# adaLN block with attention and channel mix: attention product in three fp32r parts, and the token mix split between ScalarE and VectorE

## The chip, the cores and the metric

One Trainium2 chip (trn2), one of its cores. The metric is the device time of one execution in microseconds. The kernel before took 690.93 us, the median of three runs between 690.6 and 691.36.

## The reference: what is computed

The input x is 8 batch rows of 2048 tokens of 256 numbers, all fp32. `c` (8 x 256) gives, through silu and one product with `wmod`, six vectors of 256 per batch row: shift, scale and gate for each of two halves. The reference, cut to what matters:

```python
h = _layernorm(x) * (1 + ca) + sa
qkv = h @ w_qkv + b_qkv                       # 8 heads of 64
scores = einsum('bhld,bhle->bhde', q, k) / 8  # 64 x 64 per head: attention over channels
out = einsum('bhld,bhde->bhle', v, softmax(scores)) @ w_fc + b_fc + h
x = x + ga * (layernorm(out) * gamma + beta)
h = _layernorm(x) * (1 + cb) + sb
prev = h shifted by one token, zero in front
xr = mu_r * h + (1 - mu_r) * prev
xk = mu_k * h + (1 - mu_k) * prev
x = x + gb * sigmoid(xr @ W_r.T) * (square(relu(xk @ W_k.T)) @ W_v.T)
```

## The kernel before

Since attention is over channels, everything from the layer norm to the centred output of `w_fc` and the residual is one 256 x 256 matrix m per batch row, so that the attention half is z @ m, where z is the normalised x. m comes from the Gram matrix of z over the whole batch row. The kernel therefore works on row b's second stage while it builds the Gram matrix of row n = b + 1.

The work is cut into 8 batch rows and each of these into 4 chunks (j) of 512 tokens, a chunk into 4 tiles of 128. Every engine has its own instruction stream, an order written out by hand in a function `row_steps` (row 0 with small differences, rows 1 to 6 in a loop) and `last_row` for row 7; the engines meet in semaphores. In each engine's stream a waiting instruction holds up all that is behind it. In this order PE does in a row: attention(b,0), turn_and_gram(n,0), ffn_r and ffn_k of (b-1,3), attention(b,1), ffn_out(b-1,3), turn_and_gram(n,1), turn_z2(b,0), attention(b,2), turn_and_gram(n,2), ffn_r and ffn_k (b,0), turn_z2(b,1), attention(b,3), ffn_out(b,0), turn_and_gram(n,3), turn_z2(b,2), ffn_r and ffn_k (b,1), gram_q(n), ffn_out(b,1), scores(n), ffn_r and ffn_k (b,2), wv_attn(n), turn_z2(b,3), make_m(n), ffn_out(b,2).

What happens to a chunk:
- `stats_a` (DVE, L876) and `rstd_a` (POOL, L453 to L465) give mean and inverse deviation of x; `make_z` (DVE, L886) writes z, four instructions of 255 columns.
- `turn_and_gram` (PE, L1260 and L1267) transposes z into the two PSUM banks `tr` and adds to the Gram matrix; `copy_z_t` (ACT, L620) copies the banks to `z_t`. The banks `tr` are also those of `turn_z2`.
- `attention` (PE, L1285) multiplies z_t with m_sb in fp32 into the banks `att`. It waits until DVE has read the banks of the chunk before (`t_done`).
- `squares` (ACT, L654) and `rstd_o` (POOL, L480, a pow) give the second norm, `make_x2` (DVE, L896 and L901) writes t_buf and from it x2, `stats_2` (DVE, L907) and `rstd_2` (POOL, L471 a pow, L473) the third norm, `make_z2` (ACT, L701) z2.
- `turn_z2` (PE, L1302) transposes z2, `copy_h2` (ACT, L663) writes h2 transposed into `h2t`.
- `mix` (DVE) writes dif = h2 - prev into the memory of t_buf (L930, one instruction of 1024 columns), then xr and xk by four instructions dif * mu + prev (L934).
- `ffn_r` (PE, L1318) and `take_r` (ACT, L673, tanh); `ffn_k` (PE, L1335), `take_k` (ACT, L682 relu, L684 square, L686 copy to k_hi in fp32r), `low_k` (DVE, L943) the rest k_lo; `ffn_out` (PE, L1151 to L1153) the product with w_v in three fp32r products: k_hi with the low part of the weights, k_hi with the high part, k_lo with the high part. `gate_o` (DVE, L952) and `add_y` (POOL, a DMA that adds into the output).

Once per row: `prep_base_qk` (ACT, L693, L694) and `prep_qk` (DVE, L991, L993: four instructions, each with two SBUF tensors) scale the q and k weights; `prep_wv` (POOL, L496 and L499, 1024 and 1020 columns) the v weights; `make_m` (DVE, L1026) adds the residual to the product and gives m_sb, which PE's attention of the next row and the load of the row's `ca` values by SP wait for. `take_wvf` (DVE, L972 to L977) splits the gated w_v in two fp32r parts.

Of the kernel before, what the change touches and what calls it, by code (L numbers as in the profile page):

```python
# [30 lines left out]
P = 128  # L31


def adaln_block(nc, x, w_qkv, b_qkv, w_fc, b_fc, gamma, beta, w_r, w_k, w_v, mu_r, mu_k, c, wmod, out):
# [19 lines left out]
    with ExitStack() as ctx:  # L54
# [41 lines left out]
        mu_col = sb("mu_col", [P, 2, KD])  # L96
        wv_t = sb("wv_t", [P, NP, D])
# [30 lines left out]
        m_sb = sb("m_sb", [P, KD, D])  # L128

# [3 lines left out]
        z_t = sb("z_t", [P, CH, KD, CT])  # L133
# [113 lines left out]
        m_ready = sem("m_ready")  # L247

# [7 lines left out]
        z_t_ready = sem("z_t_ready")  # L256
# [16 lines left out]
        dif_done = sem("dif_done")  # L273
# [314 lines left out]
        def _(act):  # L588
# [76 lines left out]

            def take_r(b, j, alone=False):
# [9 lines left out]
            def take_k(b, j, alone=False, halves=(0, 1)):  # L676

                i = CH * b + j
                for h in halves:
# [6 lines left out]
                    nc.scalar.activation(k_split(j)[0][:, h], k[:], ACT.Copy).then_inc(k_hi_ready, 1)  # L686
# [18 lines left out]
            def row_steps(b, first):  # L705
# [803 lines left out]
```

## Time and profile before

| what | before |
|---|---|
| median of the runs | 690.93 us |
| the profiled execution's own time | 690.6 us |
| its span, first to last instruction | 688.9 us |
| PE busy | 670.7 us (97%) |
| DVE busy | 561.0 us (81%) |
| ACT busy | 393.8 us (57%) |
| POOL busy | 317.5 us (46%) |
| TensorE clock granted, mean | 0.991 |
| attention of row 0, 1, 4 and 7 starts at | 57.98, 131.04, 371.72, 612.36 us |

A busy time is the part of the span in which the engine had an instruction in work; a PE that is busy need not be at its peak. In the timelines a line merges instructions of one kind that follow each other: start, length of the whole, engine, source line, operation, what is written from what, form, and x how many. In square brackets stands how long the engine sat idle before and whose end released it. PE's records show an fp32 product twice and an fp32r product once. Successive records overlap, so that the start of the next group, not the end of a record, tells when PE was free.

### The profile page before, as it was taken

The numbers are of one execution on the slowest core, as the hardware profiler recorded it, in microseconds if no ns is written. First come the engines' busy times: TensorE is split into PE (matmuls) and PEld (weight loads), VectorE is DVE, ScalarE is ACT, GpSimd is POOL, SyncE is SP. The second block draws the span as 40 slices with busy tenths as digits, with TensorE's granted clock in tenths as the row PEclk, the third lists the DMA queues.
The fourth block names the chain that finished last, engine by engine and source line by source line (L and its number), as shares of the span: only waits on it lengthen the run. The fifth ranks groups of instructions, "written<-read, shape, count | busy, mean of one in ns | idle before, by whom it ended". The sixth has DMA issues, their size and how long they took to land.

```text
span 688.9 us, 11754 instructions
## 1 busy us (share of the span) xinstructions
PE 670.7 (97%) x3712; PEld 539.4 (78%) x3712; DVE 561.0 (81%) x1254; ACT 393.8 (57%) x871; POOL 317.5 (46%) x520
## 2 busy tenths in 40 slices
PE   7988999999999999999999999999999999999896
PEld 6777886888778887879868887788878788687674
DVE  5693999789887998889887898979988898658973
ACT  1424575566754675474855667546754747547662
POOL 5272864573254642565335742646325753214320
PEclk9989999999999999999999999999999999999999
DMA  8849345485836666572855849366665528628225
GB/s 316 232 152 222 103 131 123 77 212 97 209 74 142 163 135 147 99 167 92 198 113 79 219 91 213 67 141 158 145 136 99 107 72 173 123 37 179 37 31 91
DMA packets 90984, 93.02 MB, mean 135 GB/s; under 512 B 4224, under 2 KB 89000, under 8 KB 90960
## 3 DMA queue, kind: packets, MB, share of 16 engines
q0 software_dynamic: 33264, 33.03, 32.6%
q1 hardware_dynamic: 55344, 55.97, 25.6%
q10 hardware_dynamic: 2352, 3.73, 1.5%
q8 instruction: 11, 0.18, 0.1%
q14 instruction: 13, 0.11, 0.0%
HBM read 42.84 MB, written 33.10 MB: 110 GB/s over the span
## 4 chain that ended last, share of the span: by engine, by line
PE 86%; DVE 7%; POOL 2%; DMA 2%; issue 1%; ACT 1%; SPq 0%; DVEq 0%; POOLq 0%
PE work L1335 14%; PE work L1318 14%; PE att L1285 13%; PE gram L1267 11%; PE gram L1398 4%; PE att L1370 4%; PE work L1151 4%; PE tr L1260 4%; PE work L1153 4%; PE work L1152 4%; PE tr L1302 4%; PE att L1389 2%; PE gram L1380 1%; PE att L1318 1%; DVE st L907 1%
## 5 line engine op out<-in xcount | busy, mean ns | idle before, releaser
L471 POOL TENSOR_TENSOR rs<-ve,neg_half 128x4 f32<-128x4 f32 x32 | 41.6, 1300 | 161.4 <-DVE ve L917 161.4
L1285 PE MATMUL att<-m_sb,z_t 128*128 128x256 f32 x496 | 112.4, 380 | 1.6 <-issue 0.8
L1335 PE MATMUL work<-mx,w_k_t 128*128 128x512 f32 x236 | 106.2, 592 | 0.0
L1285 PEld LDWEIGHTS att<-m_sb,z_t 128*128 128x128 f32 x496 | 92.4, 190 | 16.9 <-issue 5.7
L1318 PE MATMUL work<-w_r_t,mx 128*128 128x256 f32 x464 | 105.7, 381 | 0.0
L1318 PEld LDWEIGHTS work<-w_r_t,mx 128*128 128x128 f32 x464 | 85.9, 190 | 11.1
L1267 PE MATMUL gram<-z 128*128 128x256 f32 (+1 forms) x512 | 90.7, 331 | 0.0
L1267 PEld LDWEIGHTS gram<-z 128*128 128x128 f32 x512 | 81.1, 194 | 6.9
L934 DVE SCALAR_TENSOR_TENSOR mx<-t_buf,mu_col,h2t 128x512 f32<-128x512 f32 x120 | 84.3, 765 | 1.1
L654 ACT ACTIVATE sq<-att 128x256 f32<-128x256 f32 x124 | 46.1, 383 | 64.1 <-PE att L1285 64.1
L1335 PEld LDWEIGHTS work<-mx,w_k_t 128*128 128x128 f32 x236 | 44.8, 190 | 44.1 <-issue 42.6
L701 ACT ACTIVATE z<-x,nm,rs 128x256 f32<-128x256 f32 x128 | 66.5, 600 | 21.5 <-POOL nm L473 21.2
L1151 PE MATMUL work<-wvf_lo,k_hi 128*128 128x256 f32 x248 | 75.5, 304 | 1.4 <-issue 1.0
L896 DVE SCALAR_TENSOR_TENSOR t_buf<-att,rs_o,g_row 128x256 f32<-128x256 f32 x124 | 51.4, 477 | 27.8 <-POOL rs_o L480 26.9
L886 DVE TENSOR_SCALAR z<-x_in,ag_a 128x255 f32<-128x255 f32 x128 | 65.1, 570 | 5.1 <-POOL ag_a L465 3.6
L673 ACT ACTIVATE y<-work 128x512 f32<-128x512 f32 x58 | 34.5, 595 | 60.6 <-PE work L1318 60.5
L1153 PE MATMUL work<-wvf_hi,k_lo 128*128 128x256 f32 x248 | 68.9, 278 | 0.0
L1152 PE MATMUL work<-wvf_hi,k_hi 128*128 128x256 f32 x248 | 68.8, 277 | 0.0
L943 DVE TENSOR_TENSOR k_lo<-work,k_hi 128x512 fp32r<-128x512 f32 x61 | 41.2, 688 | 32.0 <-ACT k_hi L686 31.7
L663 ACT ACTIVATE h2t<-tr,mod_now 128x512 f32<-128x512 f32 x64 | 46.3, 778 | 16.0 <-PE tr L1302 16.0
L485 POOL DMA_DIRECT2D x<-in_L_attn_x_dram x32 | 55.2, 1825 | 0.0
L512 POOL DMA_DIRECT2D out_dram<-y x29 | 39.3, 1355 | 34.1 <-DVE y L952 33.7
(170 smaller groups left out, 1283.6 us busy)
## 6 DMA issues: line engine op xcount, KB each, us to landing
x_in<-in_L_attn_x_dram SPq DMA_DIRECT2D x32, 512.0 KB, 4.8
x<-rows SPq DMA_DIRECT2D x32, 512.0 KB, 3.4
x<-in_L_attn_x_dram POOLq DMA_DIRECT2D x32, 512.0 KB, 8.9
out_dram<-x SPq DMA_DIRECT2D x31, 512.0 KB, 5.1
out_dram<-y POOLq DMA_DIRECT2D x29, 512.0 KB, 6.2
rows<-row_scratch SPq DMA_DIRECT2D x16, 128.0 KB, 4.1
rows<-row_scratch SPq DMA_DIRECT2D x8, 256.0 KB, 3.8
wqkv_sb<-in_L_attn_w_qkv_dram ACTq DMA_DIRECT2D x1, 1536.0 KB, 9.7
```

What stands on the lines that cost most here:

```text
L485: nc.gpsimd.dma_start(x2[:, j], x_v[b, j], accum_op=ALU.add).then_inc(x2_filled[j], 16)
L701: ins = nc.scalar.activation(z2[:, t], x2[:, j, t], ACT.Identity, bias=nm_2[:, s, t:t + 1], scale=rs_2[:, s, t:t + 1])
L886: ins = nc.vector.tensor_scalar(z[:, j % 2, t, 0:LAST], x_in[:, j, t, 0:LAST], ag_a[:, j, 3, t:t + 1], ag_a[:, j, 7, t:t + 1], ALU.subtrac ...
L896: ins = nc.vector.scalar_tensor_tensor(t_buf[:, t], att_banks(j, alone)[t // 2][:, (t % 2) * D:(t % 2 + 1) * D], rs_o[:, s, t:t + 1], g_ro ...
L934: ins = nc.vector.scalar_tensor_tensor(dst[:, h], dif[:, h], mu_col[:, n, h:h + 1], prev[:, h], ALU.mult, ALU.add)
L1151: mm(dst, s_hi, m_lo, start=start, stop=False)
L1152: mm(dst, s_hi, m_hi, start=False, stop=False)
L1153: return mm(dst, s_lo, m_hi, start=False, stop=stop)
L1267: ins = mm(gram[:, k * D:(k + 1) * D - k * P], z[:, j % 2, t, k * P:(k + 1) * P], z[:, j % 2, t, k * P:D], start=(j == 0 and t == 0 and k ...
L1285: ins = mm(att_banks(j, alone)[q][:, (t % 2) * D:(t % 2 + 1) * D], z_t[:, j, k, t * P:(t + 1) * P], m_sb[:, k], start=(k == 0), stop=(k == ...
L1318: ins = mm(r_banks(alone)[q][:, (t % 2) * D:(t % 2 + 1) * D], mixed(j, alone)[0][:, ch, tile], w_r_t[:, ch], start=(ch == 0), stop=(ch == ...
L1335: ins = mm(k_banks(alone)[dh][:], w_k_t[:, ch, rows_dh], mixed(j, alone)[1][:, ch], start=(ch == 0), stop=(ch == KD - 1))
```

## The change

- **Attention in three products.** z_t becomes z_hi, a copy in fp32r by ACT (`copy_z_hi`), and z_lo, the rest, by DVE (`low_z`, two instructions of 512 columns per chunk, from the banks `tr`). m_sb is split by DVE into m_hi (a cast) and m_lo (a subtraction), 512 columns each, once per row. `attention` does the three products of `mm3` for each tile. Who waited for z_t_ready now waits for z_lo_ready, turn_z2 half by half.
- **The mix.** ACT writes mu * h2 into xr and xk (`scale_h2`, four instructions of 512 columns per chunk, right behind copy_h2, for j = 1 behind squares(b,3)), and DVE adds (1 - mu) * prev in place (four instructions per chunk). dif and its instruction are gone, and so are the waits of make_x2 and take_wvf for the memory shared with it. 1 - mu is worked out once (`make_rest`).
- **The order on DVE** in rows 1 to 6: make_z(n,2) and low_k(b-1,3) now stand before prep_qk(n), which stood before them.
- k_hi and k_lo have one buffer instead of two; in the last row chunks 2 and 3 use xr and xk instead of z_t, and the last k takes z_hi.

```diff
-        z_t = sb("z_t", [P, CH, KD, CT])
+        z_hi, z_lo = (part(n, [P, CH, KD, CT]) for n in ("z_hi", "z_lo"))
-        k_hi, k_lo = (part(n, [P, 2, KD, CT]) for n in ("k_hi", "k_lo"))
+        k_hi, k_lo = (part(n, [P, KD, CT]) for n in ("k_hi", "k_lo"))
...
+            def scale_h2(b, j):
+
+                i = CH * b + j
+                wait_past(act, r_done, 2 * i - 2)
+                wait_past(act, k_done, 2 * i - 2)
+                act.wait_ge(h2_ready, 2 * i + 2)
+                for n, (dst, scaled) in enumerate(zip(mixed(j), (xr_scaled, xk_scaled))):
+                    for h in range(KD):
+                        nc.scalar.activation(dst[:, h], h2t[:, h, 1 + j * CT:1 + (j + 1) * CT], ACT.Copy,
+                                             scale=mu_col[:, n, h:h + 1]).then_inc(scaled, 1)
...
                 copy_h2(b, 0)
+                scale_h2(b, 0)
...
                 copy_h2(b, 1)
                 squares(b, 3)
+                scale_h2(b, 1)
                 make_z2(b, 2)
-                copy_z_t(n, 3)
+                copy_z_hi(n, 3)
                 copy_gram(n)
                 copy_gram_low(n)
                 copy_h2(b, 2)
+                scale_h2(b, 2)
...
                 copy_h2(b, 3)
+                scale_h2(b, 3)
...
-                nc.vector.tensor_tensor(dif, h2t[:, :, 1 + j * CT:1 + (j + 1) * CT], prev, ALU.subtract).then_inc(dif_done, 1)
-                dve.wait_ge(dif_done, i + 1)
-                for n, (dst, ready) in enumerate(zip(mixed(j, alone), (xr_mixed, xk_mixed))):
+                parts = (xr_scaled, xr_mixed), (xk_scaled, xk_mixed)
+                for n, (dst, (scaled, ready)) in enumerate(zip(mixed(j), parts)):
+                    dve.wait_ge(scaled, 2 * i + 2)
                     for h in range(KD):
-                        ins = nc.vector.scalar_tensor_tensor(dst[:, h], dif[:, h], mu_col[:, n, h:h + 1], prev[:, h],
+                        ins = nc.vector.scalar_tensor_tensor(dst[:, h], prev[:, h], rest_col[:, n, h:h + 1], dst[:, h],
                                                              ALU.mult, ALU.add)
                     ins.then_inc(ready, 1)
+
+            def low_z(b, j):
+
+                i = CH * b + j
+                for h in range(KD):
+                    dve.wait_ge(z_hi_ready, 2 * i + h + 1)
+                    nc.vector.tensor_tensor(z_lo[:, j, h], tr[h][:], z_hi[:, j, h].bitcast(F32),
+                                            ALU.subtract).then_inc(z_lo_ready, 1)
...
                 nc.vector.tensor_tensor(m_sb[:].rearrange("p k d -> p (k d)"), gram[:],
-                                        res[:].rearrange("p k d -> p (k d)"), ALU.add).then_inc(m_ready, 1)
+                                        res[:].rearrange("p k d -> p (k d)"), ALU.add).then_inc(m_step, 1)
+                dve.wait_ge(m_step, 2 * b + 1)
+                nc.vector.tensor_copy(m_hi[:], m_sb[:]).then_inc(m_step, 1)
+                dve.wait_ge(m_step, 2 * b + 2)
+                nc.vector.tensor_tensor(m_lo[:], m_sb[:], m_hi[:].bitcast(F32), ALU.subtract).then_inc(m_ready, 1)
...
                 prep_now(n)
+                low_z(n, 0)
                 make_x2(b, 0)
                 stats_2(b, 0)
                 if first:
                     stats_a(n, 2)
                     stats_a(n, 3)
+                    low_z(n, 1)
                     make_x2(b, 1)
                     stats_2(b, 1)
                     make_z(n, 2)
                 else:
+                    make_z(n, 2)
+                    low_k(b - 1, 3)
                     prep_qk(n)
-                    low_k(b - 1, 3)
-                    make_z(n, 2)
+                    low_z(n, 1)
                     make_x2(b, 1)
                     stats_2(b, 1)
                 mix(b, 0)
+                low_z(n, 2)
...
                 mix(b, 1)
+                low_z(n, 3)
                 gate_o(b, 0)
...
-                            ins = mm(att_banks(j, alone)[q][:, (t % 2) * D:(t % 2 + 1) * D], z_t[:, j, k, t * P:(t + 1) * P], m_sb[:, k],
-                                     start=(k == 0), stop=(k == KD - 1))
+                            ins = mm3(att_banks(j, alone)[q][:, (t % 2) * D:(t % 2 + 1) * D],
+                                      (z_hi[:, j, k, tile], z_lo[:, j, k, tile], m_hi[:, k], m_lo[:, k]),
+                                      start=(k == 0), stop=(k == KD - 1))
...
-                elif not last and j < CH - 1:
-                    pe.wait_ge(z_t_ready, 2 * (i + 1 + CH) + 2)
-                else:
+                elif last or j == CH - 1:
                     wait_past(pe, h2_ready, 2 * i)
                 for h in range(KD):
+                    if not last and j < CH - 1:
+                        pe.wait_ge(z_lo_ready, 2 * (i + 1 + CH) + 1 + h)
```

## Rows read from the trace of the kernel before

**Rows 1.** Windows: busy us by engine, batch row 4 and the last row:
```profile
371.72:451.91 80.19, 80.16 (x451) 65.04 (x450) 68.62 (x153) 48.68 (x108) 38.53 (x63) 1.00 0.63 137
612.36:688.90 76.54, 67.21 (x338) 51.91 (x336) 54.65 (x117) 42.46 (x96) 22.68 (x23) 0.98 0.42 76
```

**Rows 2.** Timeline of PE, row 4: start us, us, engine, what, count:
```profile
371.72 3.62 PE L1285 MATMUL att<-m_sb,z_t 128*128 128x256 f32 x16
375.18 1.04 PE L1260 MATMUL tr<-ident,z 128*128 128x128 f32 x8
...
396.42 3.62 PE L1285 MATMUL att<-m_sb,z_t 128*128 128x256 f32 x16
...
406.83 3.60 PE L1335 MATMUL work<-mx,w_k_t 128*128 128x512 f32 x8
...
414.94 0.28 PE L1151 MATMUL work<-wvf_lo,k_hi 128*128 128x256 f32 x1
...
415.28 0.28 PE L1151 MATMUL work<-wvf_lo,k_hi 128*128 128x256 f32 x1
...
420.82 1.04 PE L1302 MATMUL tr<-ident,z 128*128 128x128 f32 x8
```

**Rows 3.** Timeline of ACT in row 4:
```profile
407.52 2.06 ACT L701 ACTIVATE z<-x,nm,rs 128x256 f32<-128x256 f32 x4
...
415.69 2.10 ACT L701 ACTIVATE z<-x,nm,rs 128x256 f32<-128x256 f32 x4
417.96 1.08 ACT L620 ACTIVATE z_t<-tr 128x512 f32<-128x512 f32 x2 [0.17 <-PE tr L1260]
```

**Rows 4.** Groups of ACT by line and shape: busy us, mean ns, idle before:
```profile
L663 ACT ACTIVATE h2t<-tr,mod_now 128x512 f32<-128x512 f32 x64 | 46.3, 778 | 16.0 <-PE tr L1302 16.0
...
L620 ACT ACTIVATE z_t<-tr 128x512 f32<-128x512 f32 x64 | 34.7, 598 | 30.8 <-PE tr L1260 19.2 <-issue 11.5
...
L693 ACT ACTIVATE wqk_aug<-wqk_last,neg_d 128x1024 f32<-128x1024 f32 x8 | 9.2, 1154 | 1.4 <-DVE d_now L984 1.4
...
L694 ACT ACTIVATE res<-ident_c,d_now 128x256 f32<-128x256 f32 x8 | 4.0, 500 | 0.0
```

**Rows 5.** Groups of DVE by line and shape, same columns:
```profile
L943 DVE TENSOR_TENSOR k_lo<-work,k_hi 128x512 fp32r<-128x512 f32 x61 | 41.2, 688 | 32.0 <-ACT k_hi L686 31.7
...
L930 DVE TENSOR_TENSOR t_buf<-h2t 128x1024 f32<-128x1024 f32 x32 | 39.1, 1220 | 6.0 <-ACT h2t L663 4.1 <-PE work L1318 0.8 <-DVE x L901 0.5
...
L975 DVE CAST wvf_hi<-t_buf 128x512 fp32r<-128x512 f32 x7 | 3.3, 476 | 0.2
```

**Rows 6.** Timeline of DVE in row 4:
```profile
384.69 1.28 DVE L991 SCALAR_TENSOR_TENSOR wqk_aug<-wqkv_sb,d_now,wqk_aug 128x1024 f32<-128x1024 f32 x1
...
394.14 1.66 DVE L896 SCALAR_TENSOR_TENSOR t_buf<-att,rs_o,g_row 128x256 f32<-128x256 f32 x4 [1.18 <-POOL rs_o L480]
```

**Rows 7.** Timeline of DVE at 389 us, and the second z alone:
```profile
389.08 3.88 DVE L886 TENSOR_SCALAR z<-x_in,ag_a 128x255 f32<-128x255 f32 x4
...
390.27 2.04 DVE L886 TENSOR_SCALAR z<-x_in,ag_a 128x255 f32<-128x255 f32 x1
```

**Rows 8.** Timeline of POOL in row 4:
```profile
384.87 1.99 POOL L471 TENSOR_TENSOR rs<-ve,neg_half 128x4 f32<-128x4 f32 x1 [2.70 <-DVE ve L917]
...
387.58 2.62 POOL L496 TENSOR_TENSOR wv_aug<-wv_t,rows 128x1024 f32<-128x1024 f32 x1
390.28 1.89 POOL L499 TENSOR_TENSOR wv_aug<-wv_aug 128x1020 f32<-128x1020 f32 x1
...
393.10 1.01 POOL L480 TENSOR_TENSOR rs_o<-ve_o,neg_half 128x4 f32<-128x4 f32 x1
```

**Rows 9.** Timeline of DVE at the start of row 0:
```profile
57.19 0.69 DVE L1026 TENSOR_TENSOR m_sb<-gram,res 128x512 f32<-128x512 f32 x1 [5.48 <-PE gram L1398]
...
63.81 0.15 DVE L983 TENSOR_SCALAR neg_d<-rows 128x1 f32<-128x1 f32 x1 [5.66 <-DMA rows<-row_scratch]
```

**Rows 10.** Timeline of PE at the second attention chunk of row 0:
```profile
65.79 3.69 PE L1285 MATMUL att<-m_sb,z_t 128*128 128x256 f32 x16 [0.62 <-DVE t_buf L896]
```

More of the change, by code:

```diff
@@ L162, in y_buf, with k_split, mixed @@
             return x_in[:, j] if alone else y[:, j % 2]
-        def k_split(j):
-            return k_hi[:, j % 2], k_lo[:, j % 2]
+        def k_split(j, alone):
+            return (z_hi[:, 0], z_hi[:, 1]) if alone and j == CH - 1 else (k_hi, k_lo)
         def o_banks(j, alone):
             return att if alone and j == CH - 1 else work[0:2]
-        def mixed(j, alone):
-            return (z_t[:, 2 * j - CH], z_t[:, 2 * j - CH + 1]) if alone and j >= CH // 2 else (xr[:, j % 2], xk[:, j % 2])
+        def mixed(j):
+            return xr[:, j % 2], xk[:, j % 2]
         wmod_sb = h2t[:, :, 1:1 + 6 * D]
@@ L619, in copy_z_t @@
                     act.wait_ge(z_turned, 2 * i + h + 1)
-                    nc.scalar.activation(z_t[:, j, h], tr[h][:], ACT.Copy).then_inc(z_t_ready, 1)
+                    nc.scalar.activation(z_hi[:, j, h], tr[h][:], ACT.Copy).then_inc(z_hi_ready, 1)
             def copy_gram(b):
@@ L752, in last_row @@
                 copy_h2(b, 0)
+                scale_h2(b, 0)
                 make_z2(b, 1)
@@ L755, in last_row @@
                 copy_h2(b, 1)
+                scale_h2(b, 1)
                 take_r(b, 0)
@@ L760, in last_row @@
                 copy_h2(b, 2)
+                scale_h2(b, 2)
                 take_r(b, 1, alone=True)
@@ L764, in last_row @@
                 copy_h2(b, 3)
+                scale_h2(b, 3)
                 take_r(b, 2, alone=True)
@@ L888, in make_z, with make_x2 @@
                 ins.then_inc(z_ready, 1)
-            def make_x2(b, j, mixes=None, alone=False):
+            def make_x2(b, j, alone=False):
                 i, s = CH * b + j, j % 2
-                wait_past(dve, xk_mixed, CH * b + (max(j - 1, 0) if mixes is None else mixes))
+                wait_past(dve, x2_ready, i)
                 dve.wait_ge(rs_o_ready, i + 1)
@@ L1085, in last_row @@
                 stats_2(b, 0)
[L1086 removed]
+                make_x2(b, 1, alone=True)
                 stats_2(b, 1)
                 low_k(b - 1, 3)
[L1089 to L1090 removed]
+                make_x2(b, 2, alone=True)
+                mix(b, 0)
                 gate_o(b - 1, 3)
                 stats_2(b, 2)
[L1093 to L1094 removed]
+                mix(b, 1)
+                make_x2(b, 3, alone=True)
                 take_wvf(b, alone=True)
@@ L1097, in last_row @@
                 stats_2(b, 3)
-                mix(b, 2, alone=True)
+                mix(b, 2)
                 gate_o(b, 0)
                 low_k(b, 1, alone=True)
-                mix(b, 3, alone=True)
+                mix(b, 3)
                 gate_o(b, 1, alone=True)
@@ L1116, in _ @@
             make_z(0, 1, first=True)
+            low_z(0, 0)
             stats_a(0, 3)
@@ L1120, in _ @@
             prep_now(0)
+            low_z(0, 1)
             make_z(0, 3, first=True)
@@ L1123, in _ @@
             prep_qk(0)
+            low_z(0, 2)
             rows_b()
+            low_z(0, 3)
             centre_fc()
+            make_rest()
             stats_a(1, 0)
```

71 lines of the change are left out of this document (35 added, 36 removed).

## The prediction

> **What bounds the kernel now.** I read the windows first, batch row by batch row, then the waits of PE, then the timelines of one middle row. The window of row 4 [rows 1] shows PE busy for 80.16 of its 80.19 us, DVE for 68.62 and ACT for 48.68: PE is the bound in rows 1 to 6, and everything else has slack in front of it. The last row is different: PE works 67.21 of 76.54 us, so a chain through several engines sets its end. A PE that is full says what a shorter product could give at most; what it will give is decided by how much slack each hand-over had. So I wrote down for row 4, with 371.72 as zero, when PE comes to each wait and when the buffer is ready, and did the same for the new order. The points that matter are: attention(b,2) starts at 24.70 (396.42 in [rows 2]), its bank is free when t_buf of chunk 1 is done, 394.14 + 1.66 = 395.80 or 24.08 [rows 6]; ffn_r(b,0) ends and ffn_k(b,0) starts at 35.11 (406.83), and turn_z2(b,2) starts at 49.10 (420.82) [rows 2].
>
> **PE's own work.** An attention chunk takes from 371.72 to 375.18 [rows 2], 3.46 us: 16 records of fp32. The new one is 24 records like those of lines 1151 to 1153, of which three take 415.28 - 414.94 = 0.34 us [rows 2], so 2.72 us: 0.74 less. Four chunks a row make 2.96, all 32 chunks 23.7 us. Were nothing else changed, that would be the gain.
>
> **ACT's added work.** scale_h2 is four activations per chunk, SBUF to SBUF, 512 wide, with a pointer scale. None stands in the trace. The two neighbours in kind are 1154 ns at 1024 columns and 500 ns at 256 [rows 4], a straight line between them gives 718 ns at 512; successive ones overlap by about 0.1 us (the two z_t copies of 598 ns take 1.08 together [rows 3, 4]), so 0.62 each, 2.48 for four, 9.9 us a row. Bounds: 0.49 each if it goes like the plain copy from PSUM, 0.67 if like h2t's 778 ns [rows 4]. ACT has 31.5 us a row free, so in sum it is covered; in one place it is not. After ffn_r(b,0) ACT does, without a gap, the second tanh (to 407.52), make_z2(b,1), relu, square and copy of both halves, copy_h2(b,1), squares(b,3) (to 415.69), make_z2(b,2) and then z_t for the next row's chunk 3, which waits 0.17 for PE [rows 3]. The new queue puts scale_h2(b,1) between squares(b,3) and make_z2(b,2), and turn_z2(b,2) no longer waits for the copy but for low_z, DVE's subtraction behind it. From the end of ffn_r(b,0): 0.69 + 8.17 (407.52 to 415.69) + 2.48 + 2.0 (make_z2) + 0.60 (first half of z_hi) + 0.69 (low_z, priced as k_lo [rows 5]) + 0.1 for hand-overs = 14.73 us. PE used to take 420.82 - 406.83 = 13.99, and would take 13.25. So from ffn_r(b,0) to turn_z2(b,2) the row gets 0.74 longer than before. This eats exactly the 0.74 that attention(b,2) gives between its start and ffn_r's end. What is left: **the row changes by as much as the start of attention(b,2) moves**. Behind turn_z2(b,2) I find no wait that lengthens it: m needs a cast and a subtraction more, 0.48 + 0.69 [rows 5], ready at about 79.65 in old offsets, while PE is in ffn_out(b,2) to 80.19.
>
> **The start of attention(b,2).** By PE's work alone it would move from 24.70 to 23.2. It waits for t_buf of chunk 1, which was ready 0.6 before it, at 24.08, and which does not hang on the attention product: it hangs on mix(b-1,3), the row start of DVE, POOL's chain for rs_o, then POOL's two wide operations of prep_wv. The start of this chain in the row stays (mix is four operations instead of five, 1.22 us less [rows 5], behind an m that comes 1.2 later). low_z(n,0), 1.3 us, falls in DVE's wait for rs_o(b,0). With the rest unchanged attention(b,2) starts at 24.15, 0.55 earlier.
> But the rest changes: prep_qk moves from before low_k to behind it, and make_z(n,2) in front. Today prep_qk starts at 384.69 and is past before POOL begins the wide 2.62 us at 387.58; it is make_z that runs beside it, and the rows show what happens: its four instructions take 3.88 us, the second alone 2.04, from 390.27 to just behind the end of POOL's 1.89 us operation at 392.17 [rows 7, 8]. They wait for POOL to be through. The two that are left of the four take 0.66. Conversely POOL's pow takes 1.99 beside prep_qk and 1.01 at 393.10 where DVE is idle [rows 8]: prep_qk and POOL hinder each other too. The Trainium skill says this against the change (GPSIMD Engine Reference, Key points): GpSimd shares its SBUF interfaces with VectorE, with contention for instructions in a two-port mode or with two SBUF inputs, which takes in both make_z and prep_qk. By that rule the trace agrees for make_z; for prep_qk only the 1.99 bears on it.
> From the rows, in the new order: make_z from 13.0 to 14.35, low_k(b-1,3) from 14.4 to 15.85 (its second half waits for ACT), POOL's wide operation from about 14.7 to 17.3. prep_qk's first instruction comes at 15.85 into it and ends at about 18.3. If the two engines then alternate, POOL's second wide one ends at 20.2 and prep_qk at 22.0, low_z(n,1) (1.3) at 23.3, t_buf at 24.95: attention(b,2) at 25.05, later by 0.35. If DVE goes first, prep_qk ends at 20.6 but POOL at 22.2, rs_o at 24.05, t_buf at 25.7: later by 1.1. Bounds: 23.2 (no wait at all, 1.5 earlier) and 26.2 (1.5 later). I take 0.4 later, near the alternating case, since the rows show both sides getting a turn: six rows cost 2.4 us.
>
> **Prologue and row 0.** In front of row 0 PE waits for m [rows 9], so cast and subtraction cost their 1.2 in full. low_z of the first four chunks puts 5.1 us on DVE; two of the four fall in waits for ACT and DMA, the other two, with the slack before the score softmax, push wv_attn by about 0.9. The row of ca is loaded only once m is ready, and DVE waits 5.66 for it (63.81) [rows 9]; then low_z(1,0), 1.3, stands ahead of make_x2(0,0), whose t_buf attention(0,1) waits for already now [rows 10]. It starts 3.4 later. low_z(1,1) in front of make_x2(0,1) adds 1.3, of which the shorter product and waits leave 0.6; make_z(1,2) behind it brings the first stage to 4.75 late, and ACT's chain keeps it so. Bounds 2 and 5.5; I take 4.75.
> **Last row.** The shorter products bring attention(b,2) forward by 2.2 us and its rs_o with it; mix loses the difference (1.22) but waits for ACT's scaling. Following DVE from there I keep 1.4 of it to the end; bounds 0 and 3.
>
> **Sum.** The profiled execution took 690.6 us, span 688.9, 1.7 around it; it lies 0.3 under the median 690.93. 690.6 + 4.75 + 2.4 - 1.4 = 696.35, and 0.3 to the median: **696.7 us**. A measurement of this kernel tells about 0.2%, 1.4 us, from no change.
>
> **The rivals.**
> Forecast, chance 0.40: 693 to 700.
> No port cost: prep_qk slides between POOL's operations, attention(b,2) is 0.55 earlier. 690.93 + 4.75 - 3.3 - 1.4 = 691.0, chance 0.18. For it: only make_z is seen blocked, and prep_qk's own 1.28 us is the same beside pow.
> **Faster by a quicker ACT.** Place: ACT's queue between squares(b,3) and z_hi(n,3). If scaling goes at 0.49, each row gains 0.52 more; with no port cost 1.07 a row, with prologue at 2: 690.93 + 2 - 6.4 - 1.4 = 685.1, chance 0.20. It decides at z_hi(n,3) plus low_z ready 13.25 us behind ffn_r(b,0): under that PE is the bound again.
> The waits are all absorbed, because DVE and ACT run ahead of PE more than I see: 23.7 less, 667, chance 0.07. Against it: DVE's t_buf at 24.08 in the row is fixed by engines other than PE.
> Port at its worst, 1.1 a row, start 5.5, last row 0: 690.93 + 5.5 + 6.6 = 703.0, chance 0.15.
> That the products don't get shorter is no case: the same three products run in ffn_out at 0.34 a triple.
>
> **How the numbers follow.** Faster by over 0.2%: 0.27 and 0.04 of the no-port case, 0.31. Within: 0.10, all of it from that case. Slower: 0.40 + 0.15 + 0.04 = 0.59. The range runs from the quick ACT's 685 to the worst port's 703; outside are 667 and the tails, under 0.2 together. The slower cases alone run from 693 to 703.
>
> **What would show it.** Right: attention chunks of 2.7 us; PE busy about 77 of a row of 80.6; waits of PE at turn_z2 for DVE's z_lo, and at attention for t_buf; prep_qk's group at line 991 with a mean well over 1.28 us, and z's under 0.57. Four scalings near 2.5 us. attention(0,0) some 2 us later. Wrong: a middle row under 79.5 us, or line 991 still at 1.28, or PE waiting mostly in another place, above all ffn_out for k_lo.

## The result, and the profile after

The changed kernel takes 698.39 us (median of four runs, 697.56 to 699.25) against 690.91 us of the kernel before beside it: 1.0108 times as long, 95% interval 1.009 to 1.0125. The profiled execution took 699.25 us with a span of 697.6, so 8.7 more than the span of before; between the medians it is 7.5. PE is busy for 659.2 us (before 670.7), DVE for 569.9 (561.0), ACT for 469.3 (393.8), POOL for 313.0 (317.5).

Where the 8.7 us come from is read from the starts of attention(b,0): row 0 at 59.52 (before 57.98), row 1 at 138.59 (131.04), row 7 at 621.82 (612.36). So the prologue costs 1.54, row 0 another 6.01, rows 1 to 6 together 1.91, and the last row gives 0.76 back. The first of these is the least certain: in the kernels below whose prologue is the changed kernel's, row 0 starts anywhere from 58.05 to 60.84. The windows of row 4 and of the last row, as in [rows 1] (length, then busy us of PE, weight loads, DVE, ACT, POOL, then clock, DMA share, GB/s):

```profile
380.28:460.87 80.59, 78.48 (x484) 64.74 (x482) 69.70 (x160) 57.99 (x124) 38.61 (x63) 1.00 0.62 137
621.82:697.60 75.78, 65.85 (x370) 52.88 (x368) 49.87 (x112) 52.28 (x112) 20.70 (x23) 0.95 0.43 77
```

PE, which had 0.03 us free in a row before, now has 2.11, and the row is 0.40 longer. Two of PE's waits, summed over the span (us, times, longest), name both places:

```profile
PE tr L1348 <- DVE z_lo L965: 9.5, 7, 2.8
PE att L1195 <- DVE t_buf L920: 8.2, 8, 1.4
```

The timeline of PE in row 4 shows them one by one (compare [rows 2]):

```profile
380.28 0.28 PE L1195 MATMUL att<-m_lo,z_hi 128*128 128x256 f32 x1
...
383.15 1.04 PE L1304 MATMUL tr<-ident,z 128*128 128x128 f32 x8
...
404.83 0.36 PE L1195 MATMUL att<-m_lo,z_hi 128*128 128x256 f32 x1 [1.00 <-DVE t_buf L920]
...
414.72 3.60 PE L1381 MATMUL work<-mx,w_k_t 128*128 128x512 f32 x8
...
421.90 0.28 PE L1195 MATMUL work<-wvf_lo,k_hi 128*128 128x256 f32 x1
...
424.62 1.04 PE L1304 MATMUL tr<-ident,z 128*128 128x128 f32 x8
...
429.39 1.25 PE L1348 MATMUL tr<-ident,z 128*128 128x128 f32 x8 [1.11 <-DVE z_lo L965]
```

An attention chunk takes 383.15 - 380.28 = 2.87 us instead of 3.46. Offsets in a row are counted from the start of its attention(b,0), here 380.28. Attention(b,2) starts at 24.55 in the row (before 24.70), although PE stood ready 1.00 earlier. From ffn_k(b,0) to turn_z2(b,2) it is 14.67 (before 13.99). The first wait is explained by DVE's timeline in front of it, with prep_qk in its new place (compare [rows 6]):

```profile
395.60 0.69 DVE L973 TENSOR_TENSOR k_lo<-work,k_hi 128x512 fp32r<-128x512 f32 x1 [0.48 <-ACT k_hi L701]
396.21 2.09 DVE L1020 SCALAR_TENSOR_TENSOR wqk_aug<-wqkv_sb,d_now,wqk_aug 128x1024 f32<-128x1024 f32 x1
398.22 2.10 DVE L1022 SCALAR_TENSOR_TENSOR res<-last_c,neg_d,res 128x256 f32<-128x256 f32 x1
400.25 1.27 DVE L1020 SCALAR_TENSOR_TENSOR wqk_aug<-wqkv_sb,d_now,wqk_aug 127x1024 f32<-127x1024 f32 x1
401.44 0.47 DVE L1022 SCALAR_TENSOR_TENSOR res<-last_c,neg_d,res 127x256 f32<-127x256 f32 x1
401.84 1.28 DVE L965 TENSOR_TENSOR z_lo<-tr,z_hi 128x512 fp32r<-128x512 f32 x2
403.04 1.65 DVE L920 SCALAR_TENSOR_TENSOR t_buf<-att,rs_o,g_row 128x256 f32<-128x256 f32 x4
```

and POOL's timeline beside it (compare [rows 8]):

```profile
394.81 2.41 POOL L500 TENSOR_TENSOR wv_aug<-wv_t,rows 128x1024 f32<-128x1024 f32 x1
397.29 2.75 POOL L503 TENSOR_TENSOR wv_aug<-wv_aug 128x1020 f32<-128x1020 f32 x1
```

The two engines take turns, and each seems to wait for the other to be through with a whole instruction. DVE's first one starts at 396.21, inside POOL's L500 that ends at 397.22, and ends at 398.30, 1.08 behind that, where alone it takes 1.27. POOL's L503 takes 2.75 where it takes 1.89 alone [rows 8], and ends at 400.04, 1.74 behind DVE's first. DVE's second instruction, 256 columns, needs 2.10 instead of 0.47 and ends at 400.32, 0.28 behind POOL. Each of the three ends 0.15 to 0.2 earlier than a full wait would have it, so the exclusion covers all but some 0.2 us of an instruction, as far as POOL's spans, which are rough in a profile, can tell. In DVE's groups (busy us, mean ns, idle) the two shapes of one line stand side by side: the first, 128 partitions, meets POOL in rows 1 to 6, the second, 127 partitions, does not.

```profile
L956 DVE SCALAR_TENSOR_TENSOR mx<-h2t,rest_col,mx 128x512 f32<-128x512 f32 x128 | 91.3, 775 | 18.9 <-ACT mx L678 18.9
L910 DVE TENSOR_SCALAR z<-x_in,ag_a 128x255 f32<-128x255 f32 x128 | 50.1, 453 | 4.7 <-POOL ag_a L469 3.5 <-PE gram L1311 0.9
...
L1020 DVE SCALAR_TENSOR_TENSOR wqk_aug<-wqkv_sb,d_now,wqk_aug 128x1024 f32<-128x1024 f32 x8 | 15.0, 1876 | 0.0
L1022 DVE SCALAR_TENSOR_TENSOR res<-last_c,neg_d,res 128x256 f32<-128x256 f32 x8 | 13.6, 1698 | 0.0
L1020 DVE SCALAR_TENSOR_TENSOR wqk_aug<-wqkv_sb,d_now,wqk_aug 127x1024 f32<-127x1024 f32 x8 | 10.2, 1274 | 0.0
```

The second wait comes from ACT's queue; its timeline in row 4 (compare [rows 3]) shows the scaling of chunk 1 ahead of z2 and z_hi:

```profile
423.59 2.59 ACT L678 ACTIVATE mx<-h2t,mu_col 128x512 f32<-128x512 f32 x4
426.04 2.08 ACT L716 ACTIVATE z<-x,nm,rs 128x256 f32<-128x256 f32 x4
428.00 1.09 ACT L624 ACTIVATE z_hi<-tr 128x512 fp32r<-128x512 f32 x2
```

Row 0 has a meeting of its own, which the prediction did not see. It is in the kernel before too, whose DVE and POOL timelines show mix(0,1) beside prep_wv:

```profile
95.81 4.84 DVE L934 SCALAR_TENSOR_TENSOR mx<-t_buf,mu_col,h2t 128x512 f32<-128x512 f32 x4
...
97.40 2.70 POOL L496 TENSOR_TENSOR wv_aug<-wv_t,rows 128x1024 f32<-128x1024 f32 x1
```

Four such instructions take 2.74 elsewhere, so 2.1 us were lost there already, and PE did not feel it: its turn_z2(0,2), at 99.85, needed ACT's copy and nothing that stood behind the mix on DVE. In the changed kernel the mix waits for ACT's scaling and starts 2.5 later, so that all four meet POOL, and z_lo, which turn_z2 now waits for, stands behind it. DVE's timeline there:

```profile
98.29 6.48 DVE L956 SCALAR_TENSOR_TENSOR mx<-h2t,rest_col,mx 128x512 f32<-128x512 f32 x4 [0.86 <-ACT mx L678]
104.69 1.28 DVE L965 TENSOR_TENSOR z_lo<-tr,z_hi 128x512 fp32r<-128x512 f32 x2
```

POOL's at the same time:

```profile
98.54 2.73 POOL L500 TENSOR_TENSOR wv_aug<-wv_t,rows 128x1024 f32<-128x1024 f32 x1
101.35 2.21 POOL L503 TENSOR_TENSOR wv_aug<-wv_aug 128x1020 f32<-128x1020 f32 x1
```

and PE's, which waits for the z_lo behind that mix and, inside ffn_r(0,1), for a gate_o that stands behind both (5.30 instead of 3.62):

```profile
105.52 1.16 PE L1348 MATMUL tr<-ident,z 128*128 128x128 f32 x8 [2.80 <-DVE z_lo L965]
...
106.62 5.30 PE L1364 MATMUL work<-w_r_t,mx 128*128 128x256 f32 x16
```

Turn_z2(0,2) is 5.67 late (105.52 against 99.85) where ffn_k(0,0) was 2.8 late (88.02 against 85.20).

### The profile page after: what moved, and what is told of

The parts are those of the page before. It is cut to its first block, busy times and chain, and to the rows that moved or that the text cites. A ratio compares the mean times of both kernels' runs of the same rounds, so it can differ in the third digit from the quotient of the medians.

```text
span 697.6 us, 12487 instructions
## 1 busy us (share of the span) xinstructions
PE 659.2 (94%) x3968; PEld 539.3 (77%) x3968; DVE 569.9 (82%) x1303; ACT 469.3 (67%) x999; POOL 313.0 (45%) x520
## 4 chain that ended last, share of the span: by engine, by line
PE 67%; ACT 16%; DVE 11%; issue 3%; DMA 1%; POOL 0%; ACTq 0%; DVEq 0%; POOLq 0%
PE work L1364 15%; PE work L1381 10%; PE gram L1311 7%; PE gram L1444 4%; ACT z L716 4%; PE att L1416 4%; PE tr L1348 3%; PE work L1195 2%; PE work L1196 2%; PE work L1197 2%; PE tr L1304 2%; PE att L1195 2%; ACT work L699 2%; PE att L1435 2%; DVE res L1022 2%
## 5 line engine op out<-in xcount | busy, mean ns | idle before, releaser
L1381 PE MATMUL work<-mx,w_k_t 128*128 128x512 f32 x244 | 109.9, 592 | 0.0
L1364 PE MATMUL work<-w_r_t,mx 128*128 128x256 f32 x464 | 109.0, 389 | 0.0
L475 POOL TENSOR_TENSOR rs<-ve,neg_half 128x4 f32<-128x4 f32 x32 | 37.6, 1175 | 154.2 <-DVE ve L941 154.1
L956 DVE SCALAR_TENSOR_TENSOR mx<-h2t,rest_col,mx 128x512 f32<-128x512 f32 x128 | 91.3, 775 | 18.9 <-ACT mx L678 18.9
L1364 PEld LDWEIGHTS work<-w_r_t,mx 128*128 128x128 f32 x464 | 88.2, 195 | 12.0
L678 ACT ACTIVATE mx<-h2t,mu_col 128x512 f32<-128x512 f32 x128 | 82.4, 723 | 2.8
L1195 PE MATMUL att<-m_lo,z_hi 128*128 128x256 f32 x248 | 74.2, 299 | 10.2 <-DVE t_buf L920 8.2
L1196 PE MATMUL att<-m_hi,z_hi 128*128 128x256 f32 x248 | 70.1, 283 | 0.0
L1197 PE MATMUL att<-m_hi,z_lo 128*128 128x256 f32 x248 | 70.0, 282 | 0.0
L1195 PEld LDWEIGHTS att<-m_lo,z_hi 128*128 128x128 f32 x248 | 47.3, 191 | 13.9 <-issue 13.9
```

What stands on the lines that cost most here:

```text
L678: nc.scalar.activation(dst[:, h], h2t[:, h, 1 + j * CT:1 + (j + 1) * CT], ACT.Copy, scale=mu_col[:, n, h:h + 1]).then_inc(scaled, 1)
L956: ins = nc.vector.scalar_tensor_tensor(dst[:, h], prev[:, h], rest_col[:, n, h:h + 1], dst[:, h], ALU.mult, ALU.add)
L1195: mm(dst, s_hi, m_lo, start=start, stop=False)
L1196: mm(dst, s_hi, m_hi, start=False, stop=False)
L1197: return mm(dst, s_lo, m_hi, start=False, stop=stop)
L1364: ins = mm(r_banks(alone)[q][:, (t % 2) * D:(t % 2 + 1) * D], mixed(j)[0][:, ch, tile], w_r_t[:, ch], start=(ch == 0), stop=(ch == KD - 1))
```

## The experiments

Ratios are against the kernel before, run on the same chip. In kernels that add or drop a line the line numbers shift by one or two.

**1. The two halves of the change alone.** att_only keeps the change's attention but leaves the mix as it was (dif on DVE, no scaling on ACT); mix_only puts the new mix into the kernel before.

Att_only, against the changed kernel (with the mix come back the waits of make_x2 and take_wvf for the memory that dif shares with t_buf):

```diff
-                scale_h2(b, 0)
...
+                nc.vector.tensor_tensor(dif, h2t[:, :, 1 + j * CT:1 + (j + 1) * CT], prev, ALU.subtract).then_inc(dif_done, 1)
...
-                        ins = nc.vector.scalar_tensor_tensor(dst[:, h], prev[:, h], rest_col[:, n, h:h + 1], dst[:, h],
+                        ins = nc.vector.scalar_tensor_tensor(dst[:, h], dif[:, h], mu_col[:, n, h:h + 1], prev[:, h],
```

Mix_only has the same lines with the signs turned round, against the kernel before; chunks 2 and 3 of its last row keep the memory of z_t.

> The changed kernel with the mix as it was before: dif and four scalar_tensor_tensor on DVE, no scale_h2 on ACT; the attention product, low_z, the split of m and DVE's new order stay. Theory (ACT's scaling lengthens the way from ffn_r(b,0) to turn_z2(b,2) to 14.7 us, and m's split delays the start of DVE's row): the wait of PE at turn_z2(b,2) goes (that way back to about 13.4 us), but mix(b-1,3) is 1.2 us longer again, so attention(b,2) starts about 1 us later than in the changed kernel. A middle row of 79.5 to 80.3 us and a total of 692 to 696. Rival (the loss comes from the attention split itself, the scaling is harmless): total 698 to 702, turn_z2(b,2) as late as in the changed kernel.

Measured: 705.16 us (703.79 to 705.97), ratio 1.0199 [1.0174, 1.0224]: 9 above the range, and 3 above that of the rival, which is nearer: the loss comes from the attention split. Its chain through ACT is short, as the theory has it (ffn_k(b,0) to turn_z2(b,2) 13.40), and its rows are 81.47 long all the same; row 0 is 7.2 longer than before, rows 1 to 6 together 7.5. PE's waits say why:

```profile
PE att L1175 <- DVE t_buf L900: 8.8, 9, 1.6
PE work L1344 <- DVE y L963: 5.5, 6, 0.9
PE tr L1328 <- DVE z_lo L946: 4.6, 7, 3.0
PE work L1175 <- DVE k_lo L954: 3.2, 6, 0.6
```

DVE, busy for 74.47 of an 81.0 us window of row 4, is late everywhere: ffn_r(b,0) waits inside for gate_o and takes 4.67. With the mix of before, the attention product in three parts costs 14 us; the new mix is what makes room on DVE for low_z. How much of this is the longer work of DVE and how much the waits for t_buf's memory is not separated.

> The kernel before with the new mix alone: scale_h2 on ACT at the new places, DVE adds in place; attention stays one fp32 product, DVE's order and k's two buffers as before. Theory (ACT's queue is full between ffn_r(b,0) and the copy of the next row's z, chunk 3): turn_z2(b,2) comes 14.5 us behind the end of ffn_r(b,0) in place of 13.99, so a row is 0.4 to 0.6 us longer, total 693 to 695. Rival (ACT has 31 us a row free, the scaling is hidden): row at 80.2, total 690.5 to 691.5 or a little under through the shorter mix of the last row.

Measured: 691.55 us (690.67 to 692.45), ratio 1.0005 [0.9996, 1.0015], less than expected and next to the rival's 690.5 to 691.5. Ffn_k(b,0) to turn_z2(b,2) is 14.43, as the theory has it, but rows 1 to 6 are only some 0.3 longer each, 1.9 together, of which the last row gives 0.9 back, and the total can't be told from before. So the scaling is not hidden, as the rival has it; its cost is small. The costs of the two halves, 14.3 and 0.7, do not add up to the 7.5 of both.

**2. The order on DVE.** order_old puts prep_qk back ahead of low_k and make_z.

```diff
-                    make_z(n, 2)
-                    low_k(b - 1, 3)
                     prep_qk(n)
+                    low_k(b - 1, 3)
+                    make_z(n, 2)
```

> The changed kernel with DVE's loop in the order of before: prep_qk, low_k, make_z, then low_z(n,1). Theory of the shared port: prep_qk is back at 1.28 us an instruction (now 2.09 and 2.10 for the first two), but make_z runs beside POOL's two wide operations again and takes 3.9 us in place of 1.38, and low_k comes 1.8 us later, so ffn_out(b-1,3) waits: attention(b,2) starts 0.3 to 0.6 us later, total 700 to 702. Rival (no port, the new order just came with a cost): both groups at their short times, total under 697.

Measured: 697.94 us (697.46 to 698.69), ratio 1.0099 [1.0077, 1.0121]: the changed kernel's time, not the 700 to 702 expected. Prep_qk's two lines are back at 1278 and 480 ns, and z's mean rises from 453 to 569: four of them take 3.88 beside POOL, as in [rows 7]. Attention(b,2) starts at 24.54, as in the changed kernel, and PE's wait of 1.14 stands ahead of ffn_out(b-1,3), for k_lo, instead of ahead of attention(b,2). So the new order is neither gain nor loss: it only chooses who meets POOL's wide operations.

**3. ACT's queue.** z_first puts z_hi(n,3) ahead of the scaling of chunk 1, and low_z(n,3) ahead of its mix.

```diff
                 squares(b, 3)
-                scale_h2(b, 1)
                 make_z2(b, 2)
                 copy_z_hi(n, 3)
+                scale_h2(b, 1)
...
-                mix(b, 1)
                 low_z(n, 3)
+                mix(b, 1)
```

> The changed kernel with ACT's scale_h2(b,1) behind copy_z_hi(n,3) and DVE's low_z(n,3) before mix(b,1). Theory (scaling ahead of z_hi(n,3) is what turn_z2(b,2) waits for): turn_z2(b,2) comes 13.3 to 13.5 us behind the end of ffn_r(b,0) (now 14.67); then PE waits for copy_gram behind the scaling, so of the 1.3 about 0.5 us a row stay: total 694 to 696. Rival (another wait ends at the same time): turn_z2(b,2) moves by under 0.3 us, total 698.

Measured: 690.65 us (688.76 to 692.13), ratio 0.9996 [0.9983, 1.0009], better than expected. Ffn_k(b,0) to turn_z2(b,2) is 13.39, what PE's own work takes, and rows are 79.6 to 79.8. Row 0 is 3.9 shorter: low_z(1,3) no longer stands behind mix(0,1), and turn_z2(0,2) comes at 43.28 in the row instead of 46.00. Mix(0,1) meets only the end of POOL's operations (3.30 instead of 6.48), but it also starts 3.99 later in its row, and ends later. Turn_z2(b,2) is no longer late; PE then waits up to 0.6 for ACT's copy of the Gram matrix and for xr.

**4. POOL's wide operations, moved.** row0_wv_late moves prep_wv of row 0 behind rstd_2(0,3); wv_late moves that of rows 1 to 6 behind rstd_o(b,2).

Row0_wv_late:

```diff
-                if first:
-                    prep_wv(n)
                 add_y(b, 0)
                 fill_x2(n, 0)
                 rstd_2(b, 3)
+                if first:
+                    prep_wv(n)
```

Wv_late:

```diff
-                    prep_wv(n)
                     rstd_o(b, 1)
                     rstd_2(b, 1)
                     rstd_o(b, 2)
+                    prep_wv(n)
```

> The changed kernel with POOL's two wide operations of row 0 (prep_wv) moved from before add_y(0,0) to behind rstd_2(0,3); rows 1 to 7 as they are. Theory (in row 0 they hold the port while DVE does mix(0,1), which takes 6.48 us there and 2.73 elsewhere, and low_z(1,3) and gate_o(0,0) stand behind it): mix(0,1) is back at 2.7 us, turn_z2(0,2) 2.5 to 3 us and ffn_k(0,1) 4 to 5 us earlier, row 0 at 74 to 75 us in place of 79.07, total 693 to 695. Rival (mix(0,1) is slow through something else, the added stores of ACT in the same stretch for one): row 0 stays at 79, total 698.

Measured: 696.26 us (695.81 to 697.19), ratio 1.0079 [1.0062, 1.0096], 2 less than the changed kernel where 4 to 5 were expected. Turn_z2(0,2) comes at 43.04 in the row instead of 46.00, ffn_k(0,1) at 47.60 instead of 52.25: the meeting with mix(0,1) did cost 3 to 4.6 us. But row 0 is only 3.1 shorter, 75.98: behind the wide operations stands rstd_a of the next rows, z comes late, k_lo behind it, and make_m to ffn_out(0,2) takes 5.01 instead of 3.35.

> The changed kernel with POOL's two wide operations of rows 1 to 6 moved behind rstd_o(b,2), where DVE does low_z, gate_o and take_wvf. Theory (they and prep_qk shut each other out, and t_buf of chunk 1 is late by it): the four instructions of prep_qk take 3.5 us (now 5.7), rs_o(b,1) no longer stands behind them, attention(b,2) starts at 23.4 to 23.8 in its row (now 24.55) and the row is 0.8 to 1.1 us shorter: total 691.5 to 693.5. Rival (attention(b,2) has another bound at nearly the same time): under 0.3 us a row, 696.5 to 698.

Measured: 697.33 us (695.38 to 698.35), ratio 1.0081 [1.0062, 1.01]: a miss. The time is in the rival's range, but not for the rival's reason: attention(b,2) starts at 23.20, PE's own time, so its wait was the meeting of prep_qk with POOL. The meeting only moves on to take_wvf, in DVE's timeline of row 4:

```profile
411.03 1.62 DVE L1001 TENSOR_TENSOR t_buf<-w_v_t,rows 128x512 f32<-128x512 f32 x1
412.68 2.00 DVE L1004 CAST wvf_hi<-t_buf 128x512 fp32r<-128x512 f32 x1
414.70 0.69 DVE L1006 TENSOR_TENSOR wvf_lo<-t_buf,wvf_hi 128x512 fp32r<-128x512 f32 x1
...
420.55 1.28 DVE L973 TENSOR_TENSOR k_lo<-work,k_hi 128x512 fp32r<-128x512 f32 x2
```

The product L1001 takes 0.68 and the cast 0.43 to 0.48 where POOL is quiet. Attention(b,3) then waits 0.28 for t_buf, and ffn_out(b,0) longer, in PE's timeline:

```profile
421.93 0.36 PE L1195 MATMUL work<-wvf_lo,k_hi 128*128 128x256 f32 x1 [1.49 <-issue]
```

The view names no releaser, but k_lo, which ffn_out waits for and which stands on DVE behind the late work, is done at 421.83. A row keeps only 0.5 of the 1.35.

> The changed kernel with three moves together: scale_h2(b,1) behind copy_z_hi(n,3) with low_z(n,3) before mix(b,1), prep_wv late in row 0 and late in rows 1 to 6. If the three losses are separate links of one chain their gains add: rows of 78.4 to 78.9 us, row 0 at 74 to 75, total 683 to 686, faster than both kernels. Rival (taking one away uncovers the next): 688 to 690.

Measured, experiments 3 and 4 together: 694.87 us (694.33 to 696.68), ratio 1.0058 [1.0043, 1.0074]: a miss of both ranges, worse than z_first alone. Attention(b,2) at 23.20, but attention(b,3) at 37.86, ffn_out(b,0) at 42.45 and turn_z2(b,2) at 48.85. The loss is wv_late's wait ahead of ffn_out(b,0), 1.50 here. It alone puts turn_z2(b,2) there (48.84 in wv_late); PE waits for no z_lo in the rows of either kernel. So getting z_lo early gains nothing here, while ffn_r(b,1) now comes 1.34 behind turn_z2(b,2) instead of 0.98, because ACT's copy of the Gram matrix stands behind the scaling.

Combo_split cuts the scaling and the mix of chunk 1 in combo in two:

```diff
                 copy_z_hi(n, 3)
-                scale_h2(b, 1)
+                scale_h2(b, 1, parts=(0,))
                 copy_gram(n)
+                scale_h2(b, 1, parts=(1,))
                 copy_gram_low(n)
...
                 low_z(n, 3)
-                mix(b, 1)
+                mix(b, 1, halves=(0,))
                 gate_o(b, 0)
+                mix(b, 1, halves=(1,))
```

> combo with scale_h2(b,1) and mix(b,1) cut in two: ACT scales xr, copies the Gram matrix, then scales xk; DVE mixes xr, does gate_o(b,0), then mixes xk. Theory (in the kernel with the scaling moved alone PE waits 0.6 us in each row for the copy of the Gram matrix behind the scaling): that wait goes, a row is 0.4 to 0.7 us shorter than in combo, total 679 to 683. Rival (ffn_r or ffn_k of chunk 1 then waits for the mix instead): no shorter than combo.

Measured: 698.5 us (698.1 to 699.71), ratio 1.0112 [1.0097, 1.0127]: a miss; the rival, no shorter than combo, holds. Ffn_r(b,1) does follow turn_z2(b,2) at once (48.93 to 49.91), but ffn_k(b,1) takes 4.00 until the next product instead of 3.43: its second half waits for ACT's tanh (y L689), which stands behind the scalings. In these two kernels the gains do not add; the wide operations still lie beside take_wvf on DVE, which reads two SBUF tensors and casts.

**5. POOL's wide operations where DVE leaves them alone.** After mix(b,2) DVE does k_lo (one operand in PSUM) and statistics (one operand), some 5 us, and POOL is idle. wv_quiet puts prep_wv there in every row and holds it until mix(b,2) is through; combo2 is wv_quiet with z_first; combo2_split also puts ACT's copies of the Gram matrix between the scaling of xr and that of xk, with the mix in one piece behind them.

```diff
-                    prep_wv(n)
                     rstd_o(b, 1)
...
-                if first:
-                    prep_wv(n)
                 add_y(b, 0)
                 fill_x2(n, 0)
+                pool.wait_ge(xk_mixed, CH * b + 3)
+                prep_wv(n)
                 rstd_2(b, 3)
```

> The changed kernel with POOL's two wide operations for the v weights moved in every row to behind the residual fill of the next row's chunk 0, and held there until DVE is through with mix(b,2); DVE then does k_lo and statistics, which take one SBUF tensor each. If it is the meeting of the two engines at prep_qk (and at mix(0,1) in row 0) that costs, prep_qk's 1024 wide instructions are back at 1.28 us each, attention(b,2) starts at about 23.2 in the row instead of 24.55, row 0 is about 3 us shorter, and rows 1 to 6 by about 1 each: 688 to 690.5 us. The rival, that the wide operations cost wherever they stand because POOL's small ones behind them come late (as in the two kernels that moved them before), gives 695 to 698.

Measured: 686.52 us (685.57 to 687.72), ratio 0.9923 [0.9909, 0.9937], 1.5 below the range. Rows are 79.16, row 0 74.77 (4.3 shorter), attention(b,2) at 23.20. Prep_qk's mean in DVE's groups is back:

```profile
L955 DVE SCALAR_TENSOR_TENSOR mx<-h2t,rest_col,mx 128x512 f32<-128x512 f32 x128 | 87.6, 747 | 19.1 <-ACT mx L677 19.0
...
L1019 DVE SCALAR_TENSOR_TENSOR wqk_aug<-wqkv_sb,d_now,wqk_aug 128x1024 f32<-128x1024 f32 x8 | 10.2, 1276 | 0.0
L1021 DVE SCALAR_TENSOR_TENSOR res<-last_c,neg_d,res 128x256 f32<-128x256 f32 x8 | 3.8, 479 | 0.0
```

> The same move together with z_hi(n,3) and z_lo(n,3) in front of the scaling and the mix of chunk 1. If the two delays (ACT's queue ahead of turn_z2(b,2), and the shared port ahead of attention(b,2)) are separate and each now has cover, the gains add: attention(b,2) at 23.2, turn_z2(b,2) at about 46.6, rows of 78.4, total 681 to 684 us, faster than both kernels. The rival (gains do not add, as in the kernel that put the wide operations behind rstd_o(b,2)): 688 to 692.

Measured: **681.58 us** (680.32 to 681.65), ratio 0.9849 [0.9836, 0.9862], faster than both kernels and as the theory has it. The window of row 4:

```profile
369.60:447.86 78.26, 77.81 (x483) 64.53 (x482) 67.53 (x160) 58.00 (x124) 36.63 (x63) 1.00 0.65 141
```

POOL's timeline shows the two wide operations undisturbed in the new place:

```profile
425.40 2.36 POOL L500 TENSOR_TENSOR wv_aug<-wv_t,rows 128x1024 f32<-128x1024 f32 x1 [2.26 <-DVE mx L955]
427.84 1.89 POOL L503 TENSOR_TENSOR wv_aug<-wv_aug 128x1020 f32<-128x1020 f32 x1
```

and DVE's beside them runs at its usual times (k_lo 0.69, four statistics 1.40):

```profile
426.71 0.69 DVE L972 TENSOR_TENSOR k_lo<-work,k_hi 128x512 fp32r<-128x512 f32 x1 [0.79 <-ACT k_hi L700]
427.31 1.40 DVE L930 BATCH_NORM_STATS2 st<-x 128x6 f32<-128x256 f32 x4
```

Only a small tensor_scalar at the end of POOL's second operation (neg L939) takes 0.53 instead of 0.17. PE is busy for all but 0.45 of the row: the 2.36 that four shorter chunks give (4 x 0.59) arrive as 80.19 - 78.26 = 1.93. Row 0 is still 2.6 longer than before (75.65 against 73.06); what is left there was not looked into.

> The kernel of the run before with ACT's copies of the Gram matrix between the scaling of xr and that of xk for chunk 1. PE waits there about 0.45 for the copy of the Gram matrix and then goes on to ffn_r(b,1), which needs only xr. If that wait is what is left, each row gets 0.3 to 0.45 shorter: 2 to 3 us less than the run before. If DVE's gate_o(b,0), which comes 0.8 later behind the mix of xk, sets ffn_out or the second Gram product, the time is the same or up to 2 us more.

Measured: 693.06 us (691.49 to 694.88), ratio 1.002 [1.0008, 1.0032]: 14 above the gain that was expected and 9 above the worst case. Ffn_r(b,1) starts 0.39 earlier, and its second half waits for gate_o(b,0), which stands on DVE behind the mix of xk, and that waits for ACT's later scaling. PE's timeline in row 4:

```profile
425.73 1.99 PE L1365 MATMUL work<-w_r_t,mx 128*128 128x256 f32 x8
429.25 1.99 PE L1365 MATMUL work<-w_r_t,mx 128*128 128x256 f32 x8 [1.53 <-DVE y L983]
```

**6. The same move without the change.** before_wv_quiet is the kernel before with prep_wv moved in the same way.

> The kernel before with the same move of POOL's two wide operations and nothing else: it tells whether the move alone would have made the kernel before faster, or whether it only pays together with the shorter attention product. There PE is busy for 80.16 of the 80.19 us of a row and no wait for t_buf or prep_qk stands in front of attention(b,2), so my theory gives nothing in the rows and at most some tenths in row 0: 689.5 to 691.5 us. If POOL's wide operations cost in the kernel before as well, about 1 us per row, it gives 684 to 687, and then most of what the combined kernel gains does not come from the change.

Measured: 690.23 us (689.18 to 691.79), ratio 1.0001 [0.9992, 1.0011], as expected; rows 80.18. The move alone gives nothing where PE is the bound, and 12 us (698.39 to 686.52) in the changed kernel: 8.2 in rows 1 to 6, where t_buf had become the bound, and 4.3 in row 0, where it was z_lo behind mix(0,1); the last row takes 1.4 back. So combo2's 1.5% does not come from the move by itself, and z_first's places exist only in the changed kernel. It is the change's gain, once the two things that ate it are away.

## Why the prediction came out as it did

The time (696.7 forecast, 698.39 measured) and the sign were right, and so was the mechanism in rows 1 to 6: a shorter product whose gain late buffers take back. But most of the loss lies in row 0, and most of that has a reason that the prediction does not have; some luck is in the total as well: 5.75 more was forecast and 7.5 measured between the medians (8.7 in the profiled executions). By its steps:

- **PE's own work.** 0.74 less per chunk forecast, 0.59 measured. The step took the triple at 0.34 us from ffn_out; with z as the weights a triple takes 0.35 to 0.36.
- **ACT's added work.** 718 ns and 2.48 for four forecast; 723 ns and 2.57 to 2.59 measured. The chain from ffn_k(b,0) to turn_z2(b,2) was 14.73 forecast and 14.67 measured, and z_first (13.39) shows that the place in the queue, not the amount of work, is its cause. The Trainium skill (ScalarE: Activation LUTs, What ACT_TABLE_LOAD costs) gives 186 ns + 0.833 ns per column, 93 ns more per pointer operand and an overlap of 93 ns; for 512 columns that is 706 ns, and the trace agrees within 3%.
- **The start of attention(b,2).** Forecast 0.4 later, measured 0.15 earlier. Prep_qk ran from 15.93 to 21.63 in the row (forecast 15.85 to 22.0), in the alternating case; the error is in the tail, t_buf ready at 24.4 instead of 24.95. Experiments 2, 4 and 5 show the mechanism from three sides: move either party and the wait moves with the meeting, and it goes when there is none. The Trainium skill (SBUF — State Buffer, Who interferes with whom) calls it a lock that the first to issue holds for its whole instruction, against GpSimd reads for DVE instructions with two SBUF inputs, and against casts and tensor_scalar in a two-port mode; the 2.09, 2.75 and 2.10 us above, the cast of 2.00 and the undisturbed k_lo and statistics all agree with that, up to the 0.2 us by which each ended early.
- **Behind turn_z2(b,2)** the row was forecast unchanged and is 0.39 longer (31.48 against 31.09 to its end). "I find no wait that lengthens it" is nearly true: 0.22 of it lies in turn_z2(b,2), whose second half waits for the second half of z_lo, and 0.09 each in ffn_out(b,1) and ffn_out(b,2), which run at a slower pace without a wait.
- **The row as a whole.** Rows 1 to 6 came out at 0.32 longer on average (forecast 0.4), and that is luck. In row 4 the start of attention(b,2) was 0.55 earlier than forecast, the way from there to ffn_k(b,0) got 0.52 shorter instead of 0.74, the way to turn_z2(b,2) 0.68 longer instead of 0.74, and the rest 0.39 longer instead of 0; the four errors cancel.
- **Prologue and row 0.** Forecast 4.75, measured 7.55: the term that was mis-sized. The prologue itself was forecast about 2 and took 1.54, and attention(0,1) came 1.76 late, not 3.4. The step then said that ACT's chain keeps the lateness so; in fact ffn_k(0,0) was only 2.8 late, and then mix(0,1), all of it beside POOL's prep_wv of row 0, took 6.48, with z_lo and gate_o(0,0), which PE waits for, behind it. The meeting could be read from the trace of before, where the four took 4.84 and nothing of PE's hung on them. I had weighed that meeting for prep_qk only, because prep_qk was what the diff moved, and had not asked what else was now at that time. Row0_wv_late (the mix back at 2.74, turn_z2(0,2) 2.96 earlier) and z_first (z_lo ahead of the mix, row 0 3.9 shorter) show it.
- **Last row.** Forecast 1.4 less, measured 0.76 less; not followed further.
- **The rivals.** "No port cost" fell (prep_qk's mean is 1876 ns where it meets POOL), and its 691.0 is not the time of a kernel without the meeting either: wv_quiet takes 686.52, with rows 1.05 shorter than before instead of 0.55 and a row 0 only 1.7 longer. The quicker ACT did not come (four scalings in 2.57 to 2.59, not 4 x 0.49), but its place was right, as z_first shows. The port at its worst, 1.1 a row, did not come: attention(b,2) was early. "All absorbed", 667, did not come even in combo2.

## What to carry to other kernels

When an edit frees the bounding engine, list the buffers that were ready just before they were needed (here t_buf 0.6 us ahead): they are the next bound, and what hinders them costs from then on what it did not cost before. A meeting that costs nothing today is in today's trace: mix(0,1) at 4.84 instead of 2.74 was there to be seen. GpSimd's wide operations cost nothing in the kernel before and 12 us in the changed one; beside VectorE work with one SBUF operand or a PSUM operand, held there with a wait, they cost next to nothing here. Test such edits together as well as alone: three of the combinations here lost what their parts had gained, and one kept it.

## What the runs showed of the hardware

- The fp32r product of 128x256 has more than one pace at a granted clock of 1.00. In row 4 of the changed kernel 24 of them take 2.87 us in attention (380.28 to 383.15, 119.6 ns each) and 2.72 in ffn_out(b,0) (421.90 to 424.62, 113 ns each), with the same shapes and types. The slower pace came with z_hi and z_lo as weights in every kernel here that has them, and parts of ffn_out go at 118 ns, between the two. The cause is open; no run was made on it.
- POOL's and DVE's exclusion holds by whole instructions, but for some 0.2 us, and lets the two alternate: one DVE instruction of 0.47 us took 2.10, and a POOL one of 1.89 took 2.75.
